# Attention heads stacked by DMA through a DRAM copy instead of by selection matmuls

## The reference

```python
xn = _layernorm(x, axis=-1)
qkv = xn @ w_qkv + b_qkv
q, k, v = jnp.split(qkv, 3, axis=-1)
q, k, v = (heads(q), heads(k), heads(v))            # 16 heads of 8
ctx_g = _attend(q[:, :4], k[:, :4], v[:, :4], gmask)  # causal
ctx_l = _attend(q[:, 4:], k[:, 4:], v[:, 4:], lmask)  # window of 32
s = concat(ctx_g, ctx_l) @ w_out + b_out
g = _silu(_L0_ffn_ref(xn, ...))                     # 16 experts, top 4, and a shared one
return x + s * g
```

## Time and profile before

| | us |
|---|---|
| median of 3 runs (579.01 to 580.9) | 579.53 |
| the profiled execution | 581.03 |
| its span (first to last instruction) | 579.2 |

### The profile page before, as it was taken

How to read it: one execution, slowest core, us unless ns; L and a number is a source line. 1 busy time by engine, 2 the same in 40 slices (tenths; PEclk the granted TensorE clock), 3 DMA queues, 4 the chain that set the end, 5 groups by cost and what they waited for, 6 DMA issues and landing times.

```text
span 579.2 us, 10586 instructions
## 1 busy us (share of the span) xinstructions
PE 516.5 (89%) x3930; PEld 301.7 (52%) x3960; DVE 429.8 (74%) x937; ACT 332.7 (57%) x646; POOL 179.6 (31%) x167
## 2 busy tenths in 40 slices
PE   1768999899998999899998999999998999989992
PEld 1636665555445665555445655545454755644440
DVE  6786697786698788886789788786779776877423
ACT  3544556656855457555865367564875457455851
POOL 3413431033524441024423442023342632003311
PEclk9957999998999999998999999998999999999996
DMA  9200000000000300000000300000000110000001
GB/s 233 73 1 0 2 1 1 2 1 2 0 1 2 110 2 2 1 1 1 1 2 1 94 16 3 1 1 1 1 2 0 37 38 1 3 1 0 1 1 36
DMA packets 17933, 9.82 MB, mean 17 GB/s; under 512 B 2502, under 2 KB 17754, under 8 KB 17882
## 3 DMA queue, kind: packets, MB, share of 16 engines
q1 hardware_dynamic: 17552, 8.85, 5.6%
q10 hardware_dynamic: 330, 0.30, 0.3%
HBM read 7.05 MB, written 2.10 MB: 16 GB/s over the span
## 4 chain that ended last, share of the span: by engine, by line
PE 48%; DVE 32%; issue 7%; ACT 6%; DVEq 3%; POOL 2%; DMA 1%; POOLq 0%; ACTq 0%
PE bank L746 6%; DVE kpad L1061 4%; DVE mxp L1146 4%; PE bank L629 4%; DVE mxp L1144 4%; PE bank L513 4%; PE bank L515 4%; PE bank L514 4%; PE bank L690 3%; DVE qpad L1048 3%; PE bank L659 3%; PE bank L706 3%; DVE denT L1085 3%; PE bank L730 2%; DVE hid L1100 2%
## 5 line engine op out<-in xcount | busy, mean ns | idle before, releaser
L889 ACT ACTIVATE stage<-bank 128x512 f32<-128x512 f32 (+3 forms) x240 | 112.7, 521 | 62.8 <-PE bank L663 41.7
L1220 POOL TENSOR_TENSOR hid<-hid,wrow 128x512 f32<-128x512 f32 x64 | 82.2, 1286 | 171.6 <-DVE hid L916 171.6
L1144 DVE TENSOR_REDUCE mxp<-bank 128x1 f32<-128x512 f32 (+4 forms) x192 | 89.8, 517 | 14.0 <-PE bank L632 8.2
L1100 DVE SCALAR_TENSOR_TENSOR hid<-hid,bank 128x512 f32<-128x512 f32 x72 | 48.9, 680 | 54.7 <-ACT hid L809 54.5
L746 PE MATMUL bank<-hid,down_w 128*128 128x512 f32 x144 | 76.0, 609 | 0.0
L1211 POOL TENSOR_TENSOR maxd<-mxp,k 128x512 f16<-128x512 f32 x32 | 36.4, 1137 | 117.9 <-DVE mxp L1146 64.0
L809 ACT ACTIVATE hid<-bank 128x512 f32<-128x512 f32 x72 | 43.3, 601 | 48.2 <-PE bank L515 47.4
L513 PE MATMUL bank<-xh,up_hi 128*128 128x512 f32 x144 | 60.8, 422 | 2.4 <-DVE hid L916 1.8
L514 PE MATMUL bank<-xh,up_lo 128*128 128x512 f32 x144 | 57.8, 401 | 0.0
L515 PE MATMUL bank<-xl,up_hi 128*128 128x512 f32 x144 | 57.4, 399 | 0.0
L659 PE MATMUL bank<-kpad,kall 128*128 128x512 f16 (+3 forms) x192 | 54.8, 329 | 2.1 <-ACT stage L889 1.7
(11 more groups left out here) (162 smaller groups left out, 1002.4 us busy)
## 6 DMA issues: line engine op xcount, KB each, us to landing
xin<-in_L_attn_x_dram SPq DMA_DIRECT2D x4, 512.0 KB, 4.2
xres<-in_L_attn_x_dram SPq DMA_DIRECT2D x4, 512.0 KB, 4.1
out_dram<-xres SPq DMA_DIRECT2D x8, 256.0 KB, 2.3
k<-in_c_dram SPq DMA_DIRECT2D x1, 576.0 KB, 5.8
stage<-in_L_ffn_Wg_dram SPq DMA_DIRECT2D x1, 512.0 KB, 6.0
stage<-in_L_ffn_Wu_dram SPq DMA_DIRECT2D x1, 512.0 KB, 5.9
stage<-in_L_ffn_Wd_dram SPq DMA_DIRECT2D x1, 512.0 KB, 7.4
k<-in_c_dram ACTq DMA_DIRECT2D x1, 216.5 KB, 3.9
```

Of the source, the lines that this page charges most:

```text
L889: act.activation(prob[:, t % NPROB, 0:cols], ps[:, 0:cols], ACT.Exp).then_inc(freed, 1)
L1100: dve.scalar_tensor_tensor(out=hid[:, i % NHID, :], in0=hid[:, i % NHID, :], scalar=1.0, in1=banks[at.bank(gate)][:], op0=ALU.add, op1=ALU ...
L1144: ins = dve.tensor_reduce(mxp[:, c, j:j + 1], ps[:, 0:cols], AX_X, ALU.max)
L1220: pool.tensor_tensor(hid[:, i % NHID, :], hid[:, i % NHID, :], wrow[:, iw % NWT, :], ALU.mult)\
```

## The change

The stacked strips are read from a copy of the parts in DRAM, `planes`, indexed by (2 x batch parity + tensor, head, part, dimension, token). When the second chunk of q or k has its low part, SyncE writes three parts of it (the high part twice) from `qkh` and `qkl`: six DMAs of 256 KB for each batch. The fourth part, zeros for q and ones for k, is written once for both parities at the start. The new step `strips` issues, on SyncE, one DMA each for `qtmp` and `kall` of a group, 128 rows of 2 KB each. `qtmp` gets a second buffer. `qsel` and `ksel` are gone with their matmuls, copies, PSUM tiles and the selection matrices in `c16` (2304 columns before, 256 now). In the opening VectorE makes the plane of ones with two extra operations. SyncE's writes and strips stand in its program at their place among the steps, behind or ahead of the loads and stores of x. Some waits move: the first `qpad` copy of a group waits for the strips' DMA, ScalarE's `q` and GpSimd's low part of the next batch wait until the planes of the batch before are written, and `proj` waits for the low parts, because both use the memory of `sT`. The three order strings are new throughout.

```diff
-    return ([("qsel", g, c) for c in range(NCH)] + [("ksel", g, c) for c in range(NCH)] + [("pads", g)]
-            + maxes[:half] + [("maxdone", g, 0)] + made + maxes[half:] + [("maxdone", g, 1)])
+    return ([("strips", g), ("pads", g)] + maxes[:half] + [("maxdone", g, 0)] + made + maxes[half:] + [("maxdone", g, 1)])
...
-FIRST_ORDER = ("PIPPIIIPPPIITPPITPIPTITIPPTPIPPTIPPPPPTIPPIITTVXXVXVXXVXVXVXXXVVXXVXVXX")
+FIRST_ORDER = ("PIPPIIPPPPITTPPPTTTPITTIIITIPIVIPIPPPPIPTPVXVXVXXIVXXVXXXIVXVXXVVXXX")
...
+        planes = nc.dram_tensor("planes", [4, H, PARTS, HD, S], F16)
...
-        qtmp = sb("qtmp", [P, S], F16)
+        qtmp = sb("qtmp", [P, 2, S], F16)
...
+        def written(b):
+            return 16 * (4 + 6 * b)
...
+            sp.wait_ge(plane_ready, 1)
+            for u in range(2):
+                for w, plane in enumerate((kpad[:, 1].rearrange("p j h q -> p (j h q)")[:, 0:S], maxd[:].rearrange("p j q -> p (j q)"))):
+                    sp.dma_start(planes[2 * u + w, :, PARTS - 1, :, :], plane).then_inc(planes_written, 16)
...
+                    if kind in ("q", "k") and s[1] == 1:
+                        w, to = "qk".index(kind), 2 * (at.next % 2) + "qk".index(kind)
+                        sp.wait_ge(lo_ready, at.next * 2 * NCH + (NCH + w + 1))
+                        for part, own in enumerate((qkh, qkl, qkh) if w == 0 else (qkh, qkh, qkl)):
+                            sp.dma_start(planes[to, :, part, :, :], own[:, w, :]).then_inc(planes_written, 16)
+                    elif kind == "strips":
+                        g = s[1]
+                        of, heads = b if g else at.next, slice(4 * HEADS[g], 4 * (HEADS[g] + 1))
+                        sp.wait_ge(planes_written, written(of + 1))
+                        if at.section is not FIRST:
+                            used = ("qfull", (g + 2) % HG, 1) if g != 1 else ("qfull", 0, 0)
+                            sp.wait_ge(emptied[at.bank(used)], at.taken(used))
+                            if g != 1:
+                                sp.wait_ge(kpad_ready, b * GLOBAL + (g - 1 if g else GLOBAL))
+                        for w, to in enumerate((qtmp, kall)):
+                            sp.dma_start(to[:, g % 2, :], planes[2 * (of % 2) + w, heads]
+                                         .rearrange("h a d q -> (h a d) q")).then_inc(strips_loaded[g % 2], 16)
...
-                            pe.matmul(ps[:], const16(n + "_a", g), qkh[:, w, chunk(c)], start=True, stop=False)
-                            ins = pe.matmul(ps[:], const16(n + "_b", g), qkl[:, w, chunk(c)], start=False, stop=True)
...
+                        elif at.next:
+                            act.wait_ge(planes_written, written(at.next))
...
-                    elif kind == "qsel":
-                        act.activation(qtmp[:, chunk(s[2])], ps[:], ACT.Copy).then_inc(freed, 1)
-                    elif kind == "ksel":
-                        act.activation(kall[:, s[1] % 2, chunk(s[2])], ps[:], ACT.Identity, bias=const32("onerow"))\
-                            .then_inc(freed, 1)
...
+                        act.wait_ge(lo_ready, 2 * NCH * (b + (2 if at.section is BODY else 1)))
...
-                        all_taken(dve, at, [("qsel", g, i) for i in range(NCH)])
+                        dve.wait_ge(strips_loaded[g % 2], 2 * 16 * ((b if g else at.next) * HG // 2 + g // 2 + 1))
...
+                            dve.wait_ge(k32_loaded, 16)
+                            dve.tensor_reduce(wsum[:, 0:1], ident.rearrange("p (a d) -> p a d", d=HD)[:, :, 0], AX_X, ALU.add)
+                            dve.drain()
+                            dve.tensor_scalar(maxd[:].rearrange("p j q -> p (j q)"), qpad[:].rearrange("p j h q -> p (j h q)")[:, 0:S],
+                                              wsum[:, 0:1], None, ALU.add).then_inc(plane_ready, 1)
...
+                        if at.next and c == 0:
+                            pool.wait_ge(planes_written, written(at.next))
```

More of the change, by code:

```diff
@@ L419, in build @@
         kpad_ready = sem("kpad_ready")
+        plane_ready = sem("plane_ready")
+        planes_written = sem("planes_written")
+        strips_loaded = [sem(f"strips{i}_loaded") for i in range(2)]
         qg_ready = sem("qg_ready")
@@ L485, in batch @@
                     sp.dma_start(xin[:], of_batch(x_v, b + 1)).then_inc(x_loaded, 16)
-                for c in range(NCH):
-                    sp.wait_ge(stored[c], 16 * b + 16)
-                sp.dma_start(xres[:], of_batch(x_v, b)).then_inc(xres_loaded, 16)
-                for c in range(NCH):
-                    sp.wait_ge(emptied[at.bank(("outT", c))], at.taken(("outT", c)))
-                    sp.dma_start(of_batch(out_v, b)[:, TPC * c:TPC * (c + 1), :], xres[:, TPC * c:TPC * (c + 1), :])\
-                        .then_inc(stored[c], 16)
@@ L494, in _ @@
-            for b in range(B - 1):
-                batch(At(BODY, b))
-            batch(At(LAST, B - 1))
+                if at.section is not FIRST:
+                    for c in range(NCH):
+                        sp.wait_ge(stored[c], 16 * b + 16)
+                    sp.dma_start(xres[:], of_batch(x_v, b)).then_inc(xres_loaded, 16)
+                for s in at.steps:
+                    kind = s[0]
+                    if kind in ("q", "k") and s[1] == 1:
[7 more added lines that the diff above has]
+                        sp.wait_ge(planes_written, written(of + 1))
+                        if at.section is not FIRST:
+                            used = ("qfull", (g + 2) % HG, 1) if g != 1 else ("qfull", 0, 0)
[5 more added lines that the diff above has]
+                                         .rearrange("h a d q -> (h a d) q")).then_inc(strips_loaded[g % 2], 16)
+                    elif kind == "outT":
+                        c = s[1]
+                        sp.wait_ge(emptied[at.bank(s)], at.taken(s))
+                        sp.dma_start(of_batch(out_v, b)[:, TPC * c:TPC * (c + 1), :], xres[:, TPC * c:TPC * (c + 1), :])\
+                            .then_inc(stored[c], 16)
@@ L497, in _ @@
+            sections(sp, walk)
             for c in range(NCH):
@@ L623, in walk @@
                             pe.wait_ge(qpad_ready, of * HG + (g + 1))
-                            all_taken(pe, at, [("ksel", g, i) for i in range(NCH)], at.bank(s))
                         ps = fill(at, s)
@@ L1057, in walk @@
                             continue
-                        all_taken(dve, at, [("ksel", g, i) for i in range(NCH)])
                         for h in range(4):
```

52 lines of the change are left out of this document (22 added, 30 removed).

## The result

The changed kernel takes 548.12 us in the median of 4 runs (546.42 to 548.62), the kernel before 580.21 us in the same session. The ratio is 0.9438 [0.9401, 0.9475], so 32 us are gone. The forecast was 562.2 us with a range of 549 to 574: the direction was right, the size about half of what came, and the time lies just outside the range. The profiled execution took 548.62 us.

The account below looks back on a forecast made before the run. TensorE and VectorE were taken as busiest, alternating on the chain of waits. Gains of 15.5 (selection) and 3.4 (tail) less 1.0 (strips) and 0.6 (opening) made 17.3 us: 562.2 us forecast, range 549 to 574.

Parts of the forecast that it names:

- selection's matmuls and copies out, in the order of before: Mainly heads' preparation: 128 TensorE matmuls, 27.5 us of issue, gain 15.5 us on the path; ScalarE's copies add nothing.
- new order, opening: Opening: routing moves ahead of the qpad copies, two small added VectorE operations; a loss of 0.6 us.
- new order, three repeated sections: Repeated sections: the sum had no term for the new order there.
- new order, last section: Tail: three down matmuls and the first projection move behind the last probability matmul, hidden in TensorE's waits; gain 3.4 us.
- strips' stall at the sections' start: Section start: VectorE's first qpad copy of group 1 waits 0.3 us for strips, three times; loss 1.0 us.
- ScalarE's copies at nothing: Selection's 64 copies, 41.4 us as durations, cost nothing on their own, hidden by VectorE taking qtmp later.
- my bound of +3: Opening: the upper bound, as a gain in us, around the forecast loss of 0.6; the lower was -4.
- the bound of 4: Section starts: upper bound in us on the loss from waiting for group 1's strips, charged at 1.0; lower bound 0.
- Full gain: Rival: expert matmuls fill selection's places, all 27.5 us of TensorE's time come out, 549.2 us; chance 0.21.
- VectorE is the bound all through the preparation: Rival, heads' preparation: only the selection ahead of VectorE's work counts, 8.6 us gain, 570.9 us; chance 0.18.
- The landing replaces the matmuls: Rival: a strip pair takes 9 us instead of 3.5, VectorE stalls, 22 us slower, 601 us; chance 0.10.

Follow-up runs that it names:

- e10: Order of before with strips by DMA, group 1's reads issued a section earlier, group 0's taken from the present batch's copy (wrong batch), against the kernel before: 567.02 us, 0.9771.
- e9: Changed kernel with group 1's two strip reads issued at the end of the section before, ahead of the output stores: 545.77 us, 0.94 to the kernel before.
- e4: Changed kernel with 128 matmuls of 512 columns given back to TensorE, four more in each qfull tile: 562.1 us, 0.9696 to the kernel before.
- e5: Changed kernel with 64 ScalarE copies of 128x512 given back, two with a drain ahead of each qfull copy: 566.4 us, 0.9753 to the kernel before.
- e12: Changed kernel with 64 ScalarE copies given back behind Exps of scores, reading a constant: 566.2 us, 0.9754 to the kernel before.
- e3: Changed kernel with only the opening put back in the order of before: 552.78 us, 0.9545 to the kernel before.
- e7: Changed kernel with three down matmuls and the first projection again ahead of the last probability matmul: 553.82 us, 0.9535 to the kernel before.
- e2: Kernel before's selection matmuls and copies kept, set at the place of the strips step in the new order: 574.67 us, 0.9928 to the kernel before.
- e1: Strips by DMA with every step in the order of the kernel before: 588.95 us, 1.0149 to the kernel before.
- e8: Strips by DMA in the order of before, group 0's steps from qpads to last maximum twelve steps later in repeated sections: 593.11 us, 1.0206 to the kernel before.

## Why the prediction was wrong

The way from the kernel before to the changed one, over e10 (selection out, order of before, no trips) and e9 (new order, no trip on the path), beside the terms of the sum, gains positive, in us:

| step | forecast | measured | by |
|---|---|---|---|
| selection's matmuls and copies out, in the order of before | 15.5 + 0 | 13.2 | before to e10 |
| new order, opening | -0.6 | +5.2 | e10 to e9 |
| new order, three repeated sections | 0 (no term) | 11.9 | e10 to e9 |
| new order, last section | 3.4 | 5.0 | e10 to e9 |
| strips' stall at the sections' start | -1.0 | -2.3, within noise | e9 to after |
| **sum** | **17.3** | 33.0, against 32.1 of the change | |

The first and the fifth measured term are differences of medians, the others of section lengths. The prices within the new order, each from one edit of the changed kernel, are 14.0 for the matmuls (e4), 18.3 for the copies (e5, e12), 4.7 for the opening (e3) and 5.7 for the tail (e7). With the stall they add to 40.4, more than the change, so they are not its parts: a part is worth more in the new order than in the old one. Two of them may be high as well: work given back at e4's and e5's places, with drains, costs 31.4 us, where e2 gives 28 for the whole exchange, stall included. With the old parts the new order is worth only 4 to 5 us, though its opening and tail alone are worth 10. It fits a kernel without selection.

- **Right for the order of before: what the selection is worth.** The spacing of 0.215 us instead of the listed 0.396, and the chain's share of the earlier trace rows for the part on the path, gave 15.5 us with the copies at nothing; matmuls and copies together gave 13.2 there. By the busy time it would have been 50.7. That e4 has 14.0 for the matmuls alone is no second proof, since it is another order and another place.
- **Wrong: ScalarE's copies at nothing, and no term for the new order in the repeated sections.** This is the step that failed, and the largest: 11.9 us of the 15 that the sum fell short of the change. I read the price of the removed work from the waits of the old order and then changed the order. I argued from a busy share of 80.4 of 132.7 us and from the copies' absence among the large lines of the chain, and said that VectorE's late start hid them; what they would be worth without that cover I left to a rival. In the old order the runs agree with it: 13.2 us for both parts together. In the new one 64 copies cost 18 us at two different places, and the whole exchange 28 us instead of 13. Which wait in the repeated sections makes the difference is not shown; e2 shows only that the new order gains nothing there with the selection in it. The Trainium skill, Perfetto Trace Analysis, section Identifying the Most-Contended Engine, says to optimize the engine of highest occupancy first, and that for Vector, Scalar and GpSimd occupancy is a fair measure of how close they are to their roofline. It doesn't say that work on a less occupied engine is free, and here it wasn't: ScalarE at 57% was the least occupied but one, and giving back its copies cost more than giving back TensorE's matmuls.
- **Wrong: the opening as a loss of 0.6.** I kept the sum of VectorE's work constant and so saw only the added operations. The rows after, in order of time, then the stretch of half clock in after and in before:

```profile
32.48 1.09 PE L568 MATMUL bank<-k,stage 128*128 128x128 f32 x4 [6.81 <-DVE up_lo L933]
...
34.05 0.29 DVE L1022 SCALAR_TENSOR_TENSOR cw<-msk,wsum 128x128 f32<-128x128 f32 x1
...
42.98 0.40 PE L544 MATMUL bank<-xh,up_hi 128*128 128x512 f32 x1
...
28.80:39.00 10.20, 5.69 (x25) 4.74 (x25) 8.57 (x26) 2.61 (x6) 0.00 (x0) 0.50 0.78 240
```

```profile
29.50:50.00 20.50, 14.67 (x76) 9.70 (x77) 16.20 (x50) 9.09 (x14) 3.97 (x12) 0.50 0.00 1
```

  cw is ready at 34.3 where the earlier trace rows have 44.75: 10 us sooner, not 6. The routing is no longer broken by a qpad, a kpad and maxima, and the first expert matmul comes 5 us sooner (42.98, before 48.04). TensorE waits 6.8 us for up_lo, but while the routing runs. TensorE also spends 10.2 instead of 20.5 us at the granted clock of 0.50, the 1.2 GHz level. The gain of 4.7 us (e3) is beyond my bound of +3. A part of it can be the clock: in e3 the opening's mean is 0.87 over 67.3 us, now 0.92 over 61.2, so 17.5 and 9.8 us at the lower level, and half of the difference is 3.9 us. The runs don't separate this from the earlier routing.
- **Right in mechanism, small in size: the tail.** From the sums copy to the end it is 15.4 us, 16.7 before. The projection is hidden, and the downs stand behind the sums copy:

```profile
531.42 0.60 ACT L848 ACTIVATE sums<-bank 128x512 f32<-128x512 f32 x1 [0.55 <-PE bank L709]
...
533.34 1.12 PE L738 MATMUL bank<-ctxT,wout 128*128 128x512 f32 x2
...
534.30 2.74 PE L765 MATMUL bank<-hid,down_w 128*128 128x512 f32 x6
...
538.89 1.12 PE L738 MATMUL bank<-ctxT,wout 128*128 128x512 f32 x2 [1.41 <-POOL ctxT L1248]
...
531.40:546.80 15.40, 8.32 (x22) 3.31 (x22) 6.30 (x7) 3.65 (x6) 3.93 (x4) 0.81 0.12 34
```

  TensorE now works 8.3 us of that stretch instead of 5.8, and its clock there is 0.81 instead of 0.69. That the tail itself got 1.3 us shorter is what I left out.
- **Right: the strips.** They land after 3.5 us as a pair, groups 2, 3 and 0 are hidden (no qpad copy waits for them), and only the sections' start stalls. VectorE waits 5.5 us there in four waits where I charged 1.0 in three, and the price is 2.3 us at most, within the bound of 4.
- **The rivals.** "Full gain", at 549.2, came nearest. Its condition, a new order that fills the places of selection, fits e10 against e9, and my argument against it did not hold: VectorE would have to reach 83% of a repeated section, and it reached 85%. Its price agrees by luck: it took all 27.5 us of TensorE's time and nothing of ScalarE's, where e4 and e5 have 14.0 and 18.3. "VectorE is the bound all through the preparation", at 570.9, is refuted for the new order by e4, where TensorE's work costs 14.0 us. "The landing replaces the matmuls" did not happen in the changed kernel; e1 shows that it is real for the order of before, with trips as short as forecast: there SyncE issues the pair at 163.52, and VectorE has it at 166.77. The price of the late strips there was about the waits themselves: six of 21.1 us in e1, one of 1.7 us left in e10, and 22 us between the two.

Part of the 32 us is TensorE's clock. The mean granted clock, by kernel (before, after, e12, each span beside it):

```profile
core 0: 579.2 us, clock 0.965
```

```profile
core 0: 546.8 us, clock 0.982
```

```profile
core 0: 564.4 us, clock 0.973
```

A mean of 0.965 over 579.2 us makes 40.5 us at the lower level (0.035 x 2 x 579.2), and 0.982 over 546.8 us makes 19.7. TensorE loses at most half of such time, so the clock's part is at most 10.4 of the 32 us, and in e12's 18 us at most 5.4 (30.5 us at the lower level). I did not price it. It doesn't decide the repeated sections: e2's take 133 us at the full clock, like those of before at 0.99. How much of ScalarE's 18 us is its Exps and how much the clock isn't settled further.

## What to carry to other kernels

- The price of removed work holds for the order in which it was read. Here the same work was worth 13 us in the old order and 28 in an order made without it. An engine at 57% with no large line on the chain was not free in that order: give the work back in an experiment, at two places, before costing it at nothing.
- Replacing work by a transfer is worth its engine time only if the order leaves room for the latency. The same edit was worth -1.5 points in the old order and +4.9 in the new one, and 3.8 of the 6.4 points between them came back when the data came earlier (e10). Moving one waiting step later did not help (e8).
- Issue a load when its buffer comes free, not where its consumer's step begins: here that ended VectorE's 5.5 us of waits for strips, for 2.3 us at most.

## What the runs showed of the hardware

The copy's writes to DRAM land 3.5 us after their issue, while the output's stores of the same 256 KB land after 2.3 us; the reads take 2.6 us for qtmp and 3.0 for kall, which is issued behind it. An issue costs SyncE 0.65 us for the last write and 0.33 and 0.43 for the reads in e1's rows above. The Trainium skill, DMA: Bandwidth & Descriptors, section Anatomy of one DMA, gives for another issue path 2.0 us plus bytes at 436 GB/s, an estimated 2.6 us for 256 KB, and says the completion can be late above all where the target is HBM. The read of qtmp agrees with that figure and that of kall lies 0.4 us above; of the two kinds of write to DRAM, the copy's lies 0.9 us above it and the output's 0.3 us below.

A wait can bring a slower clock behind it. In e1 TensorE is nearly idle from 162.2 to 167.2 us, and the granted clock falls behind it (columns of the earlier trace rows):

```profile
162.20:167.20 5.00, 0.89 (x3) 0.06 (x1) 0.71 (x3) 0.00 (x0) 0.00 (x0) 1.00 0.44 152
167.20:174.00 6.80, 5.06 (x34) 2.66 (x36) 6.01 (x12) 1.51 (x4) 0.73 (x1) 0.50 0.01 2
174.00:190.00 16.00, 15.09 (x100) 8.62 (x101) 13.89 (x21) 8.41 (x19) 5.95 (x6) 1.00 0.00 1
```

After 0.9 us of work in 5.0 us TensorE has 6.8 us at the 1.2 GHz level, then full clock again. The same happens once in each of the three repeated sections of e1; in the changed kernel the repeated sections have one stretch at that level, of 3.4 us, among them.
